# Macaron block on one core: weights' peaks by TensorE transposes, a reordered setup, a padded half block in down, and a refitted instruction order

## The reference

```python
x = x + 0.5 * ffn(layernorm(x), w_gate, w_up, w_down)
x = x + attn(layernorm(x), Wq, Wk, Wv, Wproj, lq1, lk1, lq2, lk2)
x = x + 0.5 * ffn(layernorm(x), w_gate, w_up, w_down)
# ffn: every input and every weight is quantised to FP4 in blocks of 16
#   h = silu(xq @ gate_q.T) * (xq @ up_q.T)      # 704 hidden units
#   return quant(h) @ down_q.T                   # back to 256
# attn: 8 pairs of heads (16 wide), rmsnorm and rotary on q and k, causal softmax over 2048,
#   attn1 - lam * attn2, times v (32 wide), layernorm per head, projection
```

## Time and profile before

| | before |
|---|---|
| time, median of 3 runs (lowest, highest) | 2341.13 us (2335.55, 2343.18) |
| the profiled execution: time, span | 2341.35 us, 2339.6 us |
| mean granted clock of PE | 0.953 |
| PE, DVE, ACT, POOL busy | 1943.9, 1835.6, 1641.9, 1435.6 us |
| setup: first instruction to the first one of the main part | 66.9 us |
| first matmul of the main part | 90.1 us |

### The profile page before, as it was taken

The page is one execution under the profiler, slowest core; times in us unless marked ns, Lnnn a source line. Parts: engine busy times, 40 slices in busy tenths (PEclk is TensorE's granted clock), DMA queues, the critical chain, the costliest instruction groups (busy, mean ns, idle before and its releaser), DMA issues. The chain is left out here.

```text
span 2339.6 us, 39570 instructions
## 1 busy us (share of the span) xinstructions
PE 1943.9 (83%) x13630; PEld 769.9 (33%) x13630; DVE 1835.6 (78%) x3862; ACT 1641.9 (70%) x2404; POOL 1435.6 (61%) x1394
## 2 busy tenths in 40 slices
PE   1376889889988988989998989889998988998855
PEld 1133333223333333333333333333332333432212
DVE  6899987758976998878976998886977998865334
ACT  2233787867878776777887777677878777788842
POOL 3567875646665676665765676665765676663313
PEclk9798999989999999999999999999999999999987
DMA  2224341322333242352333234233243223241102
GB/s 70 52 47 84 63 73 38 58 64 50 64 62 67 42 73 57 63 91 39 62 70 57 47 59 76 55 77 55 47 77 71 47 52 81 53 80 19 35 9 43
DMA packets 477493, 136.18 MB, mean 58 GB/s; under 512 B 458222, under 2 KB 477038, under 8 KB 477294
## 3 DMA queue, kind: packets, MB, share of 16 engines
q1 hardware_dynamic: 477294, 133.65, 30.5%
HBM read 11.96 MB, written 8.39 MB: 9 GB/s over the span
## 5 line engine op out<-in xcount | busy, mean ns | idle before, releaser
L1113 ACT ACTIVATE probs<-psum_s 128x1024 f32<-128x1024 f32 (+3 forms) x1280 | 1075.2, 898 | 171.5 <-PE psum_s L1410 149.0
L1371 PE MATMUL shared<-w_gu_T,xT 128*128 128x480 f16 (+1 forms) x2304 | 521.6, 375 | 110.4 <-DMA xT<-x 60.9
L1428 PE MATMUL psum_o<-probs,v_sb 128*32 128x512 f32 (+3 forms) x5120 | 590.9, 554 | 24.4 <-POOL probs L1041 15.2
L1410 PE MATMUL psum_s<-q_stack,k_stack 64*128 64x512 f16 (+3 forms) x2560 | 396.9, 357 | 121.9 <-ACT probs L1113 114.7
L1371 PEld LDWEIGHTS shared<-w_gu_T,xT 128*128 128x128 f16 x2304 | 215.6, 100 | 385.1 <-issue 126.0
L1384 PE MATMUL shared<-w_down_T,hT 128*128 128x256 f16 (+1 forms) x2176 | 294.7, 279 | 26.7 <-DVE hq L1210 14.5
L1055 ACT ACTIVATE hq<-shared,tanh_scale 128x240 f32<-128x240 f32 (+1 forms) x384 | 173.5, 457 | 184.1 <-PE shared L1371 179.1
L1410 PEld LDWEIGHTS psum_s<-q_stack,k_stack 64*128 64x128 f16 x2560 | 96.8, 94 | 547.6 <-ACT probs L1113 440.3
L1041 POOL TENSOR_SCALAR_AFFINE_SELECT probs<-probs 128x512 f32<-128x512 f32 x256 | 185.8, 731 | 136.2 <-ACT probs L1113 134.5
L1009 POOL TENSOR_TENSOR hq<-grid,qscale 128x704 f32<-128x704 f32 x128 | 184.0, 1439 | 116.2 <-DVE grid L1224 114.5
L1016 POOL TENSOR_TENSOR h<-hq,h 128x704 f16<-128x704 f32 x128 | 205.7, 1607 | 63.7 <-ACT h L1074 63.2
(11 more groups left out here) (128 smaller groups left out, 2430.4 us busy)
## 6 DMA issues: line engine op xcount, KB each, us to landing
xb<-L_attn_x SPq DMA_DIRECT2D x16, 512.0 KB, 3.8
out<-xb SPq DMA_DIRECT2D x16, 512.0 KB, 3.1
xT<-x SPq DMA_TRANSPOSE x128, 3.1
hT<-h SPq DMA_TRANSPOSE x128, 3.5
k_stack<-st_k SPq DMA_TRANSPOSE x64, 3.2
q_stack<-st_q SPq DMA_TRANSPOSE x64, 3.3
k_stack<-L_ffn_w_down SPq DMA_DIRECT2D x1, 704.0 KB, 8.3
k_stack<-L_ffn_w_gate SPq DMA_DIRECT2D x1, 480.0 KB, 4.7
```

What stands on the lines that cost most here:

```text
L1113: nc.scalar.activation(probs[:, s % 3, 2 * u:2 * u + 2, q0:CHUNK], psum_s[u][:, :, q0:CHUNK], ACT.Exp, scale=HD ** -0.5 / QK_SCALE ** 2).t ...
L1371: last = nc.tensor.matmul(bank(e)[:, 0:2 * (hi - lo)], xs[:, x, t % 2, k, :], w_gu_T[:, w, k, 2 * lo:2 * hi], start=n == 0, stop=n == len( ...
L1410: last = nc.tensor.matmul(psum_s[u][:, j, q0:CHUNK], k_stack[half, at, h, kt % NTC * P:(kt % NTC + 1) * P], q_stack[half, c % 2, h, q0:CHU ...
L1428: last = nc.tensor.matmul(psum_o[at:at + VD, q0:CHUNK], v_sb[:, kt // NTC % SLOTS * NTC + kt % NTC, 2 * g + u, :], probs[:, s % 3, 2 * u + ...
```

## The change

- **Peaks.** The columns of peaks of gate, up and down (group 0), and those of the attention weights (group 1), are transposed by PE into a PSUM row each, reduced there by DVE (`top`), and spread again to all partitions by a second PE transpose. `powers` handles a whole group. The bank `peaks` is taken from the moves, which now turn over seven.
- **Order of the setup.** Down is loaded and scaled first (`ROUNDS = (2, 0, 1)`), grid points go in the order 0, 1, 2, POOL runs `quantised_weights` 0, 1, 2 with no peaks between. The v moves come before q, k and proj; DVE only averages, POOL centres and makes the low half, ACT makes the high half. All four quarters of x are loaded in the setup, and the SP loop at the start of the main part is gone.
- **Half block.** The low weight block gets 64 rows of zeros, and the twelfth matmul of `down` uses 128 rows.
- **Order.** `spans` has 16 numbers, one for a chunk; there is a `shift` of five numbers for each chunk, added to the starts of mlp1, qkv, qk, out and mlp2; `early` goes from 0.08 to -0.5, `nudge` and `COST` have new numbers (down 2.17 to 1.97, scores' nudge -287 to -102, exp's 52 to 164).

```diff
-DUE = dict(lead=22, spans=(1014, 2922, 53, 684), tail=3915623988536360, early=0.08, mlp1=(54, 14), qkv=(-40, 42), qk=(-86, 215), out=(-629, 241), mlp2=(171, 33),
+DUE = dict(lead=22086547, spans=(23222, 1510, 102, 673, 5470, 37, 53, 833, 3886, 3470, 7, 846114, 7956, 5815, 146, 4544), tail=2275384895397277466624, early=-0.5, mlp1=(-97, 32), qkv=(-40, 18), qk=(16, 299), out=(-471, 59), mlp2=(121, 55), shift=(...),
...
-        at.append(at[-1] + due["spans"][c % NCH])
+        at.append(at[-1] + due["spans"][c])
...
-        mlp(0, tiles, s0 + due["mlp1"][0] * k, due["mlp1"][1] * k, (0, c))
+        mlp(0, tiles, s0 + (due["mlp1"][0] + due["shift"][c][0]) * k, due["mlp1"][1] * k, (0, c))
...
+            first_v = len(moves)
+            for k in range(KC):
+                moves.append((3, [w_att[:, 2, r, k * P:(k + 1) * P] for r in range(KC)], P, wv_full[:, k, :], None))
...
             banks = [psum_s[0][:, 0], psum_s[0][:, 1], psum_s[1][:, 0], psum_s[1][:, 1],
-                     psum_o, *shared]
+                     psum_o, *shared[0:BANKS - 1]]
+            NB = len(banks)
+            peaks = shared[BANKS - 1]
+            ROUNDS = (2, 0, 1)
+            groups = ((0, 3, 0), (3, 5, 256))
...
-                    sp.dma_start(xb[:, 0:NTC, :], x_v[0][:, 0:NTC, :]).then_inc(x_loaded[0], 16)
+                    for c in range(NCH):
+                        sp.dma_start(xb[:, c * NTC:(c + 1) * NTC, :], x_v[0][:, c * NTC:(c + 1) * NTC, :])\
+                            .then_inc(x_loaded[c], 16)
...
+                    nc.gpsimd.memset(w_down_T[:, 2 * KD + 1, :], 0.0).then_inc(fills_done, 1)
+                    nc.gpsimd.memset(minus_half[:, :], -0.5).then_inc(fills_done, 1)
                     nc.gpsimd.memset(v_sb[:, :, :, :], 1.0).then_inc(fills_done, 1)
-                    nc.gpsimd.memset(minus_half[:, :], -0.5).then_inc(fills_done, 1)
...
                     for m in range(3):
-                        peak(m)
-                    for m in range(2):
                         quantised_weights(m)
-                    for m in (3, 4):
-                        peak(m)
-                    quantised_weights(2)
+
+                    wv_T = wv_full[:, :, :].rearrange("p k (h d) -> p k h d", d=VD)
+                    pool.wait_ge(v_meaned, 1)
+                    for k in range(KC):
+                        nc.gpsimd.tensor_tensor(wv_T[:, k], wv_T[:, k],
+                                                v_mean[:, k].unsqueeze(2).broadcast_to([P, NH, VD]), ALU.subtract)\
+                            .then_inc(v_centred, 1)
+                    for k in range(KC):
+                        high, low = (w_qkv_T[:, i, k, 2 * C:3 * C] for i in range(2))
+                        pool.wait_ge(v_centred, k + 1)
+                        pool.wait_ge(v_high, k + 1)
+                        nc.gpsimd.tensor_tensor(low, wv_full[:, k, :], high, ALU.subtract).then_inc(v_low, 1)
...
+                    def top(g):
+                        lo, hi, at = groups[g]
+                        dve.wait_ge(w_peak_row, g + 1)
+                        nc.vector.tensor_reduce(w_top[0:hi - lo, g:g + 1], peaks[0:hi - lo, at:at + P], AX_X, ALU.max)\
+                            .then_inc(w_top_ready, 1)
...
-                    scaled_weights(0)
-                    scaled_weights(1)
+                    for m in ROUNDS:
+                        scaled_weights(m)
                     grid_points(0)
+                    top(0)
+                    grid_points(1)
                     powers(0)
-                    scaled_weights(2)
-                    grid_points(1)
-                    powers(1)
                     attention_peaks()
                     low_parts(0)
                     grid_points(2)
-                    powers(2)
+                    top(1)
                     low_parts(1)
+                    powers(1)
...
+                    def peak_rows(g):
+                        lo, hi, at = groups[g]
+                        n = hi - lo
+                        pe.wait_ge(w_peak_ready, hi)
+                        nc.tensor.transpose(peaks[0:n, at:at + P], w_peak[:, lo:hi], ident[:, :]).then_inc(w_peak_row, 1)
+                        pe.wait_ge(w_top_ready, g + 1)
+                        nc.tensor.transpose(peaks[:, at + P:at + P + n], w_top[0:n, g:g + 1].broadcast_to([n, P]),
+                                            ident[0:n, 0:n]).then_inc(w_peak_all, 1)
+
+                    peak_rows(0)
                     seen = -1
                     for n, (m, srcs, height, high, low) in enumerate(moves):
                         if m != seen:
+                            if m == 2:
+                                peak_rows(1)
...
+                    for k in range(KC):
+                        act.wait_ge(v_centred, k + 1)
+                        nc.scalar.activation(w_qkv_T[:, 0, k, 2 * C:3 * C], wv_full[:, k, :], ACT.Copy).then_inc(v_high, 1)
...
-                    for c in range(1, NCH):
-                        load(c)
...
-                            parts += [(KD, P, 2 * KD), (KD, HALF, 2 * KD + 1)]
+                            parts += [(KD, P, 2 * KD), (KD, P, 2 * KD + 1)]
```

More of the change, by code:

```diff
@@ L51 @@
 SLOTS = NCH + 1
[L56 to L65 removed]
+DUE = dict(lead=22086547, spans=(23222, 1510, 102, 673, 5470, 37, 53, 833, 3886, 3470, 7, 846114, 7956, 5815, 146, 4544), tail=2275384895397277466624, early=-0.5, mlp1=(-97, 32), qkv=(-40, 18), qk=(16, 299), out=(-471, 59), mlp2=(121, 55), shift=((0, -1, 16, 24, 13), (-7, 98, 143, 42, -12), (2, 36, 11, 12, 3), (9, -20, 9, -3, -2), (189, 0, 11, 37, -70), (64, 31, -4, 27, 185), (0, 36, 6, 88, -16), (-77, -7, 13, -11, -17), (96, -15, -18, 0, 29), (34, 0, -22, 26, 23), (-12, 10, -3, -6, 9), (-20, 22, 9, -27, -37), (14, -6, -6, -7, 13), (-12, 16, 35, 7, -6), (-74, 111, 47, 0, -5), (104, 20, -9, -26, 0)),
+           nudge=dict(add_down=-123, add_out=-3, copy_o=-6, copy_xT=-55, dequant_h=34, dequant_x=3,
+                      divide_h=-8, divide_x=2, exp=164, gate=15, grid_h=-6, grid_x=45,
+                      head_stats=-2, heads_out=5, hidden=-5, high_h=-72, high_qk=-10, load=5,
+                      low_h=-3, low_qk=5, low_x=11, mask=-9, norm_heads=-9, norm_qk=43, norm_x=50,
+                      points_h=40, points_x=-5, project_out=2, project_qk=-1, project_v=-1,
+                      quant_h=-9, quant_x=-4, read_qk=-2, read_v=36, rms=-1, rope_add=-25, rstd=-3,
+                      scores=-102, square_h=-1, square_x=-24, stats=10, tanh=-4, transpose_o=39,
+                      transpose_x=-26, turn_h=-18, turn_qk=1, turn_x=-18, values=-1))
 ST = 2
@@ L697, in grid_points, with powers @@
                         dve.wait_ge(w_rounded, m + 1)
[L699 to L704, removed]
+                    def top(g):
[3 more added lines that the diff above has]
+                            .then_inc(w_top_ready, 1)
+                    def powers(g):
+                        lo, hi, at = groups[g]
+                        dve.wait_ge(w_peak_all, g + 1)
+                        pw, inv = (w_pow[:, i, lo:hi] for i in range(2))
+                        wait(done(nc.vector.tensor_scalar(pw.bitcast(U32), peaks[:, at + P:at + P + hi - lo].bitcast(U32),
+                                                          23, None, ALU.logical_shift_right)))
                         wait(done(nc.vector.tensor_scalar(inv.bitcast(I32), pw.bitcast(I32), -float(2 ** 23),
@@ L739, in _ @@
                                                              w_pow[:, 0, 2:3], ALU.mult, ALU.mult)))
-                    powers(3)
-                    powers(4)
+                    dve.wait_ge(fills_done, 1)
                     low_parts(2)
+                    dve.wait_ge(w_high_done, first_v + KC)
+                    wv_T = wv_full[:, :, :].rearrange("p k (h d) -> p k h d", d=VD)
+                    wait(done(nc.vector.tensor_reduce(v_mean[:, :, :], wv_T, AX_X, ALU.add)))
+                    nc.vector.tensor_scalar(v_mean[:, :, :], v_mean[:, :, :], 1.0 / VD, None, ALU.mult).then_inc(v_meaned, 1)
                     low_parts(3)
@@ L757, in _ @@
                     wait(done(nc.vector.tensor_scalar(neg_lam[:, :], neg_lam[:, :], -LAMBDA_INIT, None, ALU.add)))
[L760 to L768, removed]
-                        wait(done(nc.vector.tensor_tensor(low, wv_full[:, k, :], high, ALU.subtract)))
                 @block.tensor
@@ L781, in _ @@
                             seen = m
-                        if n >= 8:
-                            split = [low is not None for _, _, _, _, low in moves[:n - 7]]
+                        if n >= NB:
+                            split = [low is not None for _, _, _, _, low in moves[:n - NB + 1]]
                             if split[-1]:
```

78 lines of the change are left out of this document (39 added, 39 removed).

## The result

| | before | changed kernel |
|---|---|---|
| time, median | 2338.54 us (5 runs) | 2354.67 us (5 runs) |
| ratio to before, 95% interval | | 1.0072 [1.0052, 1.0091] |
| span of the profiled execution | 2339.6 us | 2354.8 us |
| first statistics of the main part | 66.91 us | 57.33 us |
| first quantisation | 74.32 us | 62.91 us |

The account below looks back on a forecast made before the run. DVE was taken to bound the start and mostly PE the long middle, after a setup nothing overlaps. From 2341 us, 16.5 (setup and start), 14 (padding) and 11 (order) were subtracted: 2300 us, range 2272 to 2326.

Parts of the forecast that it names:

- The setup: Before the main part: removing peak instructions and reordering ends the setup at 51.8 instead of 66.4, gaining 14.6 us.
- All four passages of POOL: Setup: POOL's switches between ordinary work and the peak instruction, about 6 us standing each; the change removes all four.
- the fill: Setup: POOL's zero fill and the `v_sb` fill behind it end long before POOL's first product at 25, costing nothing.
- the tail: End of the setup: DVE's work after ACT's last copy shrinks from 5.0 us to 2.6 us.
- the bound that I had kept open: Setup: at most 7.07 us before POOL's first product might remain, making the gain 10.9 us.
- The start: Start of the main part: loading all x in the setup removes DVE's wait for the second quarter, 1.9 us.
- The half block: Twelfth matmul of down: padding to 128 rows spares PE 25.6 us, of which 14 us reach the end.
- the one from the chain: Middle: PE lines are 54.9% of a chain stretch, so that share of PE's saving was taken to reach the end.
- The refitted order: Middle 2000 us: new order bounded by best and worst windows, 32 us gained to 28 lost; 11 us gain taken.
- the good end: Middle 2000 us: if the new order were everywhere as good as the best window, 32 us would be gained.
- A sign that the prediction had named: Middle: the prediction is wrong if PE's idle time grows by the 25 us that padding frees.
- The rival "slower": Refitted order issues `scores` while their bank isn't free, PE waits 0.63 us for exp each time; chance 0.12, 0.05 within 0.3%.

Follow-up runs that it names:

- reordered setup: On the changed kernel with the order of before, DVE's attention peaks and powers moved ahead of the second matrix's grid points in the setup: 2320.66 us.
- without the exclusion of `grid` and `points`: DVE's 384 grid and points instructions replaced by reductions: 2239.05 us with new setup, padding and order of before; 2248.75 us in the changed kernel.
- a kernel of 2326 us: The changed kernel with the order of before (old DUE, COST and due times), keeping new setup and padded half block: 2326.22 us, ratio 0.9934.

## Why the prediction was wrong

**The setup, forecast 14.6 us: mis-sized, the mechanism right.** All four passages of POOL went. The main part's first statistics came 9.6 us earlier. The missing 5.0 us are two terms of my sum: the second instruction of up's grid pass was taken as 1.76 us and took 4.25, and the powers after it were taken as 0.6 in all and took 3.1. Both were given the durations of rows in which POOL had been silent, at a time where I had myself put POOL's product. The reordered setup got 4.3 us of them back. That the two make up the whole 5.0 is partly luck, since smaller terms were off too and cancelled. DVE started at 5.73 instead of 7.1, but then its first 128x96 scaling step took 1.37 us instead of 0.21 and ended at 8.89, just behind POOL's fill of `v_sb` (4.46 to 8.83): the fill that the forecast had put at nothing. The low parts took 0.4 less than forecast, and the tail 0.6 more, 0.4 of it in the scaling of the rotary table, 0.90 us instead of 0.47 with POOL at work beside it. A passage before the first product, the bound that I had kept open, isn't there: 0.08 us.

**The start, forecast 1.9 us: right.** From the first statistics to the first quantisation it was 5.6 us instead of 7.4. Together they give 11.4 us by the trace, and the setup alone measured 15 (11 to 19).

**The half block, forecast 14 us: the cost right, what comes of it wrong.** In the changed kernel a down is as short as forecast:

```profile
1423.05 2.03 PE L1416 MATMUL shared<-w_down_T,hT 128*128 128x256 f16 x17
1424.92 1.38 PE L1403 MATMUL shared<-w_gu_T,xT 128*128 128x480 f16 x6
```

It is 1.87 us from its start to the next work's. PE was spared 20.7 us (25.6 forecast), of which 0 to 4 arrive. The step that failed here is the one from the chain: that 54.9% of a chain lie on an engine doesn't mean that such a share of a saving passes through. The chain shows who was last at each point, and not how close behind the next one came; how close that was wasn't read.

**The refitted order, forecast a gain of 11 us: this is the step that failed, and it turned the sign.** It costs 27 us (23 to 31). I had bounded it by the best and worst windows of PE under the old order (32 gained, 28 lost) and then took a third of the good end, for which the rows gave no reason. And I judged an order by idle time of PE, as if the durations of all instructions were fixed whatever the order. They aren't: with the order alone changed the same instructions take 11.5 us more on DVE and 11.5 more on POOL, and without the exclusion of `grid` and `points` two thirds of the loss are gone. Why this order loses by it stays open, as said above. A sign that the prediction had named came true: in the middle 2000 us PE's idle time grew by more than the 25 us, from 226.0 to 262.1. The rival "slower" named the wrong mechanism. The waits for exp became 197 instead of 175 but shorter, 102.5 us instead of 109.8, and never came near 235.

**The chances.** Slower by over 0.3% had 0.07. The profile of before already held the warning: `points` on a 512-wide tile took 1148 ns in the median with a least of 627, with hardly any wait shown (1.4 us before 64 of them), and a plan whose table of costs carries such a mean as a constant has no way to see what it does to it.

## What to carry to other kernels

Before a duration is taken from a row into a new place, compare the least and the mean of that group: where they lie apart and the instruction shows no wait, its length is likely set by its neighbours, as here. Beside POOL's products put those instructions of DVE that are reductions or have an input in PSUM, and keep those with two tiles in SBUF apart from them; if an order is fitted by a table of costs, price the exclusion in it. A saving on an engine that isn't the only one short of room is worth a fraction of itself, here 0 to 7 of some 20 us.

## What the runs showed of the hardware that I had not expected

DVE's and POOL's exclusion cost more than anything that the change touched: with grid and points out of it, a kernel of 2326 us takes 2239. It isn't only for large tiles: an instruction with three elements in a row took 2.68 us at 31.25, until POOL's product ended, where in the reordered setup the same one took 0.17. An input in PSUM is another matter. These are rows of the changed kernel:

```profile
42.64 2.80 POOL L649 TENSOR_TENSOR k_stack<-k_stack,hq 128x1536 f32<-128x1536 f32 x1 [8.74 <-DVE k_stack L713]
...
45.02 0.14 DVE L729 TENSOR_SCALAR hq<-shared 128x2 uint32<-128x2 uint32 x1
```

That step reads PSUM and ran inside POOL's product at its full speed, and so did the low parts ahead of it (four in 1.55 us from 43.17, as in the kernel before). The next step, with its input in SBUF, took 0.28 us instead of 0.17 and ended at 45.47, just behind the product (45.44).
